# Attention scores one place earlier in a vision tower's slot, and four token passes moved between TensorE's fill-ins

## The reference

```python
tokens = einsum('bpi,hi->bph', patches, W) + b          # 128 images x 64 patches x 2352 -> 128
h = concat([cls, tokens]) * pos_embed
# attention block on x = layernorm(h); each position is a sequence of 128 images
value = relu(x @ Wv.T + bv)
ema   = relu(damped_ema(x) + x * omega)                  # four scans along the images
base  = ema @ Wmx.T + bmx                                # residual gate, qk, attention gate, intermediate
scores = (qk*w0 + b0) * QK**-0.5 @ (qk*w1 + b1).T + relative_bias
w     = softmax(scores) @ value
out   = layernorm(x + sigmoid(base[..., :128]) * (relu(inter + (w * gate) @ Wh.T + bh) - x)) * ln_w + ln_b
h = h + out
# mixture of experts on layernorm(h): logits = x @ Wr, softmax over all tokens,
# each of 8 experts takes its 1024 best tokens, two layers with gelu, weighted, added to h
```

## Time and profile before

| | us |
|---|---|
| median of 3 runs | 955.01 |
| lowest, highest | 953.62, 955.89 |
| profiled execution, its own time | 960.5 |
| its span | 958.4 |
| TensorE busy | 766.0 |
| VectorE busy | 561.4 |
| ScalarE busy | 445.5 |
| GpSimd busy | 477.1 |

### The profile page before, as it was taken

How to read it: one execution, slowest core, us unless ns; L and a number is a source line. 1 busy time by engine, 2 the same in 40 slices (tenths; PEclk the granted TensorE clock), 3 DMA queues, 4 the chain that set the end, 5 groups by cost and what they waited for, 6 DMA issues and landing times.

```text
span 958.4 us, 13714 instructions
## 1 busy us (share of the span) xinstructions
PE 766.0 (80%) x4819; PEld 595.1 (62%) x4819; DVE 561.4 (59%) x1239; ACT 445.5 (46%) x733; POOL 477.1 (50%) x478
## 2 busy tenths in 40 slices
PE   1799999999999999999999966443167999788771
PEld 1799888878887887888888754131124554444330
DVE  1303687788788778777877865944877433321110
ACT  2553666666756666665676624210550233222220
POOL 2314554555445546455544512441103578887885
PEclk9899999999999999999999996856557899888896
DMA  9977999998898898889889210000101133433432
GB/s 225 211 174 175 214 211 207 212 205 203 198 221 193 204 219 198 195 200 216 193 202 219 76 56 22 11 12 22 11 4 24 29 63 59 64 62 65 67 40 25
DMA packets 135057, 124.71 MB, mean 130 GB/s; under 512 B 17385, under 2 KB 125793, under 8 KB 134861
## 3 DMA queue, kind: packets, MB, share of 16 engines
q1 hardware_dynamic: 113600, 91.27, 41.7%
q0 software_dynamic: 18848, 31.58, 17.4%
q10 hardware_dynamic: 2540, 0.99, 0.5%
HBM read 87.99 MB, written 12.98 MB: 105 GB/s over the span
## 4 chain that ended last, share of the span: by engine, by line
DVE 27%; PE 23%; POOL 22%; issue 16%; ACT 6%; DMA 3%; ACTq 1%; another core or an unknown queue 0%; SPq 0%; DVEq 0%; POOLq 0%
POOL out L641 10%; PE bank L1397 9%; POOL XS L631 6%; DVE Y L993 4%; PE bank L1503 3%; DVE stats L943 3%; DVE XR L935 3%; DVE O L935 3%; DVE QT L1067 3%; ACT XS L844 2%; POOL rsB L512 2%; ACT S L800 2%; PE bank L1488 2%; POOL rsC L512 2%; PE bank L1534 2%
## 5 line engine op out<-in xcount | busy, mean ns | idle before, releaser
L1397 PEld LDWEIGHTS bank<-XS,WT 126*128 126x128 f32 (+1 forms) x2432 | 303.6, 191 | 20.7 <-issue 20.0
L1397 PE MATMUL bank<-XS,WT 126*128 126x128 f32 (+1 forms) x2432 | 310.5, 283 | 6.1 <-issue 6.1
L697 ACT ACTIVATE XS<-XS 84x1152 f32<-84x1152 f32 (+1 forms) x192 | 184.4, 1032 | 0.0
L588 POOL COPY XS<-XS 84x1152 f32<-84x1152 f32 x64 | 91.3, 1427 | 62.9 <-PE bank L1397 32.1
L641 POOL DMA_INDIRECT out<-XS x64 | 105.4, 1647 | 27.2 <-issue 18.7
L631 POOL DMA_INDIRECT XS<-token_rows,XS x64 | 65.4, 1022 | 54.8 <-DVE XS L1270 35.9
L993 DVE TENSOR_TENSOR_SCAN Y<-qdec,XT 128x512 f32<-128x512 f32 (+1 forms) x68 | 78.3, 1173 | 2.5 <-ACT XT L733 2.5
L873 ACT ACTIVATE XS<-bank,VT 128x512 f32<-128x512 f32 x64 | 43.8, 688 | 70.4 <-PE bank L1615 70.4
L601 POOL DMA_DIRECT2D XS<-XS x118 | 66.4, 565 | 17.3 <-POOL XS L588 17.3
L1615 PE MATMUL bank<-XS 128*128 128x512 f32 x128 | 68.8, 687 | 1.1 <-ACT XS L733 0.8
L999 DVE SCALAR_TENSOR_TENSOR ET<-Y,ema_c,ET 128x512 f32<-128x512 f32 (+1 forms) x68 | 62.7, 922 | 1.8
(11 more groups left out here) (243 smaller groups left out, 1332.1 us busy)
## 6 DMA issues: line engine op xcount, KB each, us to landing
XS<-in_x SPq DMA_DIRECT2D x192, 392.0 KB
XS<-XS POOLq DMA_DIRECT2D x118, 189.0 KB, 7.5
out<-O SPq DMA_DIRECT2D x16, 256.0 KB, 9.7
token_rows<-XR SPq DMA_DIRECT2D x16, 256.0 KB, 8.6
XS<-in_L_ffn_W SPq DMA_DIRECT2D x16, 256.0 KB
XS<-in_L_tok_W SPq DMA_DIRECT2D x1, 1176.0 KB, 9.3
XS<-token_rows,XS POOLq DMA_INDIRECT x65, 3.7
out<-XS POOLq DMA_INDIRECT x64
```

The lines of the kernel that those rows point to most:

```text
L588: pool.tensor_copy(ST[0:ROWS, n % 2, :, :, :].rearrange("p m j r -> p m r j"), px[:, :, :, PASSES:PATCH])\
L697: ins = act.activation(area(slice(0, ROWS), k // 4, piece, m0, m0 + CCOL // 2).rearrange("p m j r -> p m r j"), px[:, :, :, REST * piece:m ...
L1397: ins = pe.matmul(TOK[half][:, c0:c0 + CCOL], weights, pixels, start=(t == 0), stop=(t == passes_of(n) - 1))
```

## The change

Stage S, the score products with the VectorE's part behind them, is taken out of the head of the slot, where it served group b, and put near the end of the slot before, where the same group is still "a": behind Q and K, ahead of R. K moves with it, from behind R to ahead of S. Of the four passes behind Q, two go behind V, one behind L and one behind I; the total stays 76.

```diff
-        SLOT = ["S b", "C 0 3", "w 0", "T a", "U b", "C 0 0", "Z b", "P b", "N a", "K 0", "X a", "E a", "C 0 1", "C 0 2",
+        SLOT = ["C 0 3", "w 0", "T a", "U b", "C 0 0", "Z b", "P b", "N a", "K 0", "X a", "E a", "C 0 1", "C 0 2",
                 "W 0", "O b", "C 1 3", "w 1", "C 1 0", "A a", "H b", "C 1 1", "C 1 2", "W 1", "V a", "C 2 3", "w 2",
                 "J b", "L b", "C 2 0", "C 2 1", "C 2 2", "W 2", "c a", "Y b", "C 3 3", "w 3", "d a", "F a", "M b",
-                "D a", "I a", "C 3 0", "C 3 1", "C 3 2", "W 3", "v a", "Q b", "R b", "K 1"]
+                "D a", "I a", "C 3 0", "C 3 1", "C 3 2", "W 3", "v a", "Q b", "K 1", "S a", "R b"]
...
-            FILL = {"T": 15, "P": 4, "V": 13, "L": 20, "D": 4, "I": 16, "Q": 4}
+            FILL = {"T": 15, "P": 4, "V": 15, "L": 21, "D": 4, "I": 17}
```

## The result

| | before | changed |
|---|---|---|
| median of 10 runs, us | 954.27 | 950.09 |
| lowest, highest | 951.34, 960.14 | 947.19, 952.98 |
| profiled execution, its span | 958.4 | 948.4 |

The ratio is 0.9952, 95% interval 0.9931 to 0.9974: 4.2 us between the medians, 4.6 by the ratio. The forecast was 940, a gain of 15.6 us. The direction was right, the size was three times too large, and 950.09 lies outside the range of 936 to 948.

A forecast was written before the change was run, and what follows sets the result against it. Each slot was bound by the VectorE up to the router's transposes, then by TensorE's queue. Gains of 12 x 0.92 = 11.0, 1.8 and 2.8 made 15.6 us, taking 955.0 to 939.4, said as 940; range 936 to 948.

The forecast's parts named there:

- The VectorE's chain from O to Q, 24.47 us with 0.66 us of waits left: Weighted sum's first product to router's transposes: VectorE's chain stays 24.47 us, TensorE's waits fall from 1.62 to 0.66.
- x: New TensorE wait at the last chunk's first pass for POOL-issued copies to land: 0.1 to 1.6 us, mean 0.4.
- Router at 25.81 + x: Router's products start 25.81 us after the weighted sum's first product, plus the landing wait, which delays them.
- the copy X: ScalarE copy the router's products need, done 25.77 us after the weighted sum's first product; 0.98 us of scores cover it.
- the second rival: Loads packed 3% tighter land the copy 0.5 us later on average: 945 us, up to 949; chance 0.20.
- X ... comes 0.26 earlier: After the token transposes, normalised X is ready at 5.4 us, TensorE needs it at 5.5: no new wait.
- three signs of being wrong: VectorE's stretch grows beyond the landing wait, POOL's chunk copies wait for loads, or X reaches TensorE after the token transposes.
- The slot, 32.96: Average of the twelve full slots after the change, landing wait included: 32.96 us, a gain of 0.92 each.
- The ends: Slot ahead of the twelve gains nothing; two slots where passes end gain 0.9 us each; the last group gains 2.8.
- no change: Rival: a 0.1 us fit fails, VectorE's chain grows, the slot stays near 33.8: 955 us; chance 0.04.
- the score add behind the row's token step: VectorE's chain meets the score add there and grows, the mechanism named in the no-change rival; chance 0.04.
- three fits of 0.1 us: Scores covering the ScalarE copy, softmax product ahead of its transposes, X ahead of TensorE: each in time by 0.1 us.

The follow-up runs named there:

- e3: New order of stages with the passes left at their old places, against the kernel before: 958.64 us, ratio 0.9986.
- e4: Old order of stages with the passes at their new places, against the kernel before: 970.55 us, ratio 1.0100.
- e9: Changed kernel with two passes more ahead of the last gate products and two less behind; 956.53 us, 1.0005 of the kernel before.
- e2: Changed kernel with the VectorE dividing only 8 of 128 softmax columns, work left out; 948.23 us, 0.9879 of the kernel before.
- e6: Changed kernel with the softmax division held until POOL has added epsilon for the next group; 946.71 us, 0.9900 of the kernel before.
- e7: Changed kernel with the last chunk begun behind the gate products and the division held behind POOL's epsilon; 937.18 us, 0.9812 of the kernel before.
- e12: Repeat, in the next group of runs, of the changed kernel with later last chunk and held division; 936.22 us, 0.9809 of the kernel before.
- e5: The changed kernel measured again with no edit, on a second chip; 948.15 us, 0.9928 of the kernel before.

## Why the prediction was wrong, point by point

- **The VectorE's chain from O to Q, 24.47 us with 0.66 us of waits left**: right. Q stands at O + 24.5 to 25.5, the excess being the slots in which x reaches it.
- **Router at 25.81 + x**: right, 26.32 against 26.31 in the slot shown. The scores cover the copy X but for 0.1 to 0.2 us; e3 and e4 show that passes and scores are worth something only together, and e9 the slope in x.
- **The landing wait x, mean 0.42**: right in kind, a little small. Over the twelve slots it is 0.32 to 1.36, mean 0.56. The copies landed at O + 18.0 to 19.0, before at 17.9 to 19.4, so the second rival (loads packed tighter) did not come true; the matmuls resumed 0.13 us behind the landing in all twelve, a step I had put at zero, and that is the whole excess.
- **"X ... comes 0.26 earlier, 5.4, against TensorE's 5.5. Both fit by 0.1 us, so I count no new wait there"**: this step failed. I moved the VectorE's instructions up and kept POOL's root at its duration of before. With the scores' addition and maximum out of the way the division starts 0.17 us ahead of the root in place of 0.13 behind it, the root takes 1.43 us in place of 1.04, X ends 5.79 us after the start of the token transposes in place of the 5.4 forecast, and its transposes start at 5.85 in place of 5.5. That is 0.38 us a slot. Shown by e2 (division short) and e6 (division later), both of which bring 1.04 back. The forecast's own terms held the meeting: the root at 3.43 - 0.26 = 3.17 us after the token transposes, the division at 3.9 - 0.69 = 3.2. The trace of before held its price, 0.3 us in the one slot that was 0.7 us longer, which the forecast named and did not follow. None of the forecast's three signs of being wrong came up, since none was about X's own transposes.
- **The slot, 32.96**: measured 33.66. Worked out: 0.38 from the root, 0.14 from x, 0.09 and 0.04 from router to token transposes and from these to H; the last 0.05 are two slots whose stretch behind the token transposes was 0.41 and 0.13 longer than in the others. The gain fell short by only 0.61, since the slot of before was taken as 33.88 and is 33.97 on the mean. e7 and e12, with root and landing wait gone, have 32.86 and 32.99.
- **The ends**: the tail was about right, 5.3 against 4.6 (4.3 in e5). The softmax chain of the last group is 3.3 us shorter against 2.8 forecast: Q at 631.55, exponentials at 636.00, so 4.45 us in place of 638.91 - 631.11 = 7.80. They start right behind the copy of the router's result, as worked out. The slot ahead of the twelve, put at nothing, lost 0.45 us.

The timeline of the ScalarE at the last group:

```profile
635.91 0.20 ACT L733 ACTIVATE LG<-bank 128x32 f32<-128x32 f32 x1 [2.62 <-PE bank L1534]
636.00 0.39 ACT L800 ACTIVATE S<-S,nmax 128x128 f32<-128x128 f32 x1
```

In sum: 3.7 + 4.3 to 5.3 less 0.5 makes 7.5 to 8.5 us where the clock did not fall; 2.6 less where it did, and the later first pass, whose cause is not known, takes up to 1.0 more, so about 4 to 8. The two measurements are 4.6 us (0.9952) and 6.9 us (0.9928). The 7 us missing in the slots (twelve times 0.61 between the slot's gain of 0.31 and the 0.92 forecast) are the larger part of the error. Of the rivals, "no change" came nearest in the slots: it had one of the three fits of 0.1 us fail, and the slot near 33.8. But it gave another mechanism for it (the score add behind the row's token step), left the gain at the ends out of its 955 us, and had a chance of only 0.04.

Whether one instruction for addition and root together would avoid the clash was not tried.

## What to carry to other kernels

A fit of 0.1 us between two engines isn't a fit: write down which instructions then start side by side, and price each by what the other does to it, since moving one instruction by 0.3 us changed another's duration by 0.4. A pass is free only up to the first product whose consumer is on the critical chain, so place fill-ins by what is queued behind them and not by the long stand they lie in. When a large move gives little, look for more than one loss: cut the slot at an instruction between them, read each stretch by itself, and undo them one at a time and then together. Here the ratio went from 0.9928 to 0.9812 in one group with two small edits. A slot that is longer than its neighbours before the change may be the next loss in small: look at it first.

## What the hardware showed

- A VectorE instruction with two operands in SBUF holds up POOL's 128 x 4 root when it starts first, and 0.3 us in the order of their starts decide it. The root takes 1.04 us when it meets none, and also when the VectorE's 0.69 us division starts 0.07 us (one slot of e4) to 0.23 us behind it; that division kept its 0.69. When the division started first, the root was longer by what was left of the division, less 0.13 to 0.14 us: 1.54 us with the division 0.05 us ahead (the slot behind the twelve in the kernel before, and two slots of e4), 1.43 with 0.17, 1.36 with 0.23, and 1.04 with 0.86, when it was over. The same holds for line 999 (0.75 us, two operands in SBUF): it starts 0.07 us ahead of the root for rsB in all twelve slots of both kernels, and that root takes 1.58 us.
- With one operand in PSUM the root was not held: the VectorE's evacuation of the value products (line 986, 0.68 us, PSUM and SBUF) starts 0.02 us ahead of the root for rsC in the same slots, and that root takes 1.05 us.
- The larger pair pays on the VectorE's side: line 1067 takes 1.77 us beside POOL's copy and 0.68 without it, the scans 3.36 and 2.33. The copy had 1.24 us left when line 1067 started, which came out 1.09 us longer.
- The Trainium skill (SBUF — State Buffer, "SBUF: two separate sides") says that a VectorE instruction with two SBUF inputs and a GpSimd instruction that reads SBUF take a shared pair of ports as a lock, whoever starts first, for the whole instruction. The roots that wait for the division and for line 999, the one beside line 986 that does not, and line 1067 beside the copy agree with it but for the 0.13 to 0.15 us. The division that started behind the root and lost nothing does not: the root seems to hold the ports for a part of its length only. That last is argued from these durations and not shown.
- The granted clock may fall to 0.50 after the same short idle in one execution and stay at 1.00 in the next of the same kernel: 6.42 against 3.83 us for 30 matmuls. In e4 it fell behind three of twelve waits of 1.0 us.
- The kernel before has medians of 954.3, 955.2, 959.7 and 954.7 us in four measurements. The third is of another chip than the second and the fourth, and those 5 us are more than this change gives, so only kernels run on one chip were compared.
